# Feed-forward entry of the last two layers: where the shifts, the statistics and the turns stand in the order of the attention steps

## The reference, cut to what matters

```
h = shift_token(x)                       # upper 64 channels come from the token before
q, k, v = split(h @ wqkv); q, k = l2norm * scale, rotated
o = local_attention(q, k, v)             # windows of 64, 8 heads of 64
x = x + o @ wo
h = shift_token(x)                       # <- the feed-forward entry begins here
h = (h - mean(h)) / sqrt(var(h) + 1e-5) * lg + lb
a, g = split(h @ w1 + b1);  x = x + (a * gelu(g)) @ w2 + b2
```

## Time and profile before

| | us |
|---|---|
| median of 3 runs (lowest, highest) | 1318.48 (1316.27, 1319.15) |
| profiled execution, its own time | 1316.07 |
| span of the profiled execution | 1314.3 |
| busy: TensorE, VectorE, ScalarE, GpSimd | 1193.9, 989.3, 799.1, 387.0 |

### The profile page before, as it was taken

The page is one execution under the profiler, slowest core; times in us unless marked ns, Lnnn a source line. Parts: engine busy times, 40 slices in busy tenths (PEclk is TensorE's granted clock), DMA queues, the critical chain, the costliest instruction groups (busy, mean ns, idle before and its releaser), DMA issues.

```text
span 1314.3 us, 21968 instructions
## 1 busy us (share of the span) xinstructions
PE 1193.9 (91%) x7921; PEld 684.2 (52%) x7921; DVE 989.3 (75%) x2058; ACT 799.1 (61%) x1585; POOL 387.0 (29%) x304
## 2 busy tenths in 40 slices
PE   6799999999999879896899999998889979799987
PEld 4366666666666634342333333343567754477653
DVE  5878978889779268778566677675789857888855
ACT  5866867767768223240466666676668862688751
POOL 0000000001000035475300000014588842698823
PEclk9899999999999899996699999998989999899999
DMA  5576757767767636661323311100111100011101
GB/s 154 128 164 156 179 132 169 169 149 164 165 156 168 154 112 144 140 210 59 100 59 100 77 38 40 27 18 7 33 25 34 34 18 0 21 34 34 32 11 32
DMA packets 62824, 119.92 MB, mean 91 GB/s; under 512 B 15523, under 2 KB 30061, under 8 KB 61325
## 3 DMA queue, kind: packets, MB, share of 16 engines
q1 hardware_dynamic: 62716, 118.53, 37.6%
HBM read 37.68 MB, written 5.57 MB: 33 GB/s over the span
## 4 chain that ended last, share of the span: by engine, by line
PE 71%; DVE 14%; ACT 5%; issue 4%; POOL 2%; SPq 2%; DMA 2%; POOLq 0%; DVEq 0%; ACTq 0%
PE ps L750 15%; PE ps L770 8%; PE ps L1070 6%; PE ps L1029 5%; PE ps L1050 4%; PE ps L1127 4%; SPq L563 2%; PE ps L721 2%; PE ps L1178 2%; PE ps L1261 2%; PE ps L1200 2%; PE ps L1232 2%; ACT probsT L2260 2%; PE ps L902 2%; PE ps L892 2%
## 5 line engine op out<-in xcount | busy, mean ns | idle before, releaser
L2260 ACT ACTIVATE probsT<-ps 128x512 f32<-128x512 f32 (+1 forms) x304 | 164.0, 577 | 100.7 <-PE ps L1054 89.9
L1471 DVE TENSOR_REDUCE negmax<-ps 128x1 f32<-128x1024 f32 x128 | 153.5, 1204 | 40.6 <-PE ps L770 40.3
L2446 POOL TENSOR_SCALAR rstd<-mv 128x4 f32<-128x4 f32 (+1 forms) x31 | 7.1, 230 | 507.8 <-DVE mv L1405 507.6
L770 PE MATMUL ps<-k_st,q_st 64*128 64x512 f32 x512 | 130.7, 630 | 9.8 <-ACT d_sq L2105 5.3
L1029 PE MATMUL ps<-arena 84*128 84x512 bf16 (+3 forms) x384 | 113.7, 357 | 24.8 <-DVE cmax L1718 22.7
L2105 ACT ACTIVATE d_sq<-ps,negmax 128x1024 f32<-128x1024 f32 x86 | 95.9, 1115 | 62.1 <-DVE negmax L1471 59.4
L1718 DVE CUSTOM_DVE_ANT_0 q_st<-ps,rel 128x256 f32<-128x256 f32 (+7 forms) x128 | 96.7, 755 | 42.9 <-PE ps L1029 42.1
L750 PE MATMUL ps<-probsT,v_nat 128*128 128x256 f32 x512 | 121.3, 391 | 5.2 <-DMA probsT<-probs 3.1
L1718 DVE CUSTOM_DVE_ANT_0 k_st<-ps,rel 128x256 f32<-128x256 f32 (+7 forms) x128 | 96.8, 756 | 38.5 <-PE ps L1029 37.1
L750 PE MATMUL ps<-probsT,v_st 128*128 128x256 f32 x512 | 119.3, 385 | 1.0 <-DVE xn L1424 0.6
L1050 PE MATMUL ps<-arena 87*128 87x512 bf16 (+3 forms) x384 | 112.7, 337 | 5.5 <-ACT probsT L2260 3.3
(11 more groups left out here) (232 smaller groups left out, 2542.5 us busy)
## 6 DMA issues: line engine op xcount, KB each, us to landing
probsT<-arena SPq DMA_DIRECT2D x336, 128.0 KB, 2.4
probsT<-probs SPq DMA_DIRECT2D x176, 128.0 KB, 2.4
d_sq<-e_gates SPq DMA_DIRECT2D x16, 512.0 KB, 5.3
probsT<-probsT SPq DMA_DIRECT2D x62, 128.0 KB, 2.5
arena<-c_q_parts SPq DMA_DIRECT2D x8, 576.0 KB
arena<-c_k_parts SPq DMA_DIRECT2D x8, 576.0 KB
q_st<-e_gates SPq DMA_DIRECT2D x8, 512.0 KB, 5.2
k_st<-e_gates SPq DMA_DIRECT2D x8, 512.0 KB, 5.8
```

Of the source, the lines that this page charges most:

```text
L770: ins = pe.matmul(ps[:, pair(m, 4 + 2 * i + head) + n, :], q_st[r:r + R0, i * P:(i + 1) * P], k_st[r:r + R0, n * CH:(n + 1) * CH], start=T ...
L1471: dve.tensor_reduce(negmax[:, u:u + 1], s2, AX_X, ALU.max, negate=True).then_inc(s_a_negmax, 1)
L2260: act.activation(c_p[:, kt % 2, j0:j0 + heads, q0 - kt * P:q0 - kt * P + n], ps[:, 4 + c % 2, 0:heads * n].rearrange("p (h n) -> p h n", n ...
```

## The change

In each of the two layers (l = 0 and 1):

- VectorE: `shift` of chunks 0 and 1 moves from steps 12 and 13 to steps 10 and 11, in the same place inside the step.
- VectorE: both `ffn_stats` move from the end of step 14 to its head, before the row maximum of tile 14 (a new argument `begin`). `ffn_xn` of chunk 0 stays at the end of step 14; that of chunk 1 moves into step 15, behind nm8 of tile 15 (a new argument `early`).
- TensorE: `ffn_turn` of chunk 0 moves from ahead of step 15 to inside it (behind the scores), that of chunk 1 from inside step 15 to behind it.
- ScalarE: `ffn_yT` of chunk 0 moves inside step 15 from ahead of the copy of v to behind it (`held`), that of chunk 1 to behind the exponentials of tile 15.

No instruction is added or removed. GpSimd's and SyncE's streams stay as they are.

```diff
@@ TensorE, loop over the layers
                 ffn_in(l, 0, 0)
                 ffn_in(l, 1, 1)
                 step(l, 14)
-                ffn_turn(l, 0, 0)
-                step(l, 15, lambda: ffn_turn(l, 1, 1))
+                step(l, 15, lambda: ffn_turn(l, 0, 0))
+                ffn_turn(l, 1, 1)
                 up(l, 0)
                 up(l, 1)
                 step(l, 16)
@@ VectorE, step
-            def step(l, t, piece=None):
+            def step(l, t, piece=None, begin=None, early=None):
                     n, par = TILES * l + t, t % 2
 
+                    if begin:
+                        begin()
                     if exists(t, 2) and n:
                         rotate(l, t + 2)
...
                                                  op0=ALU.mult, op1=ALU.mult).then_inc(s_d_nm8, 1)
+                    if early:
+                        early()
                     if exists(t, -1):
                         dve.wait_ge(s_d_pt, n)
@@ VectorE, loop over the layers
-                for t in range(12):
-                    if l == 0:
+                for t in range(14):
+                    if l == 0 and t < 6:
                         step(l, t, lambda: second_batch(t))
+                    elif t in (10, 11):
+                        step(l, t, lambda: shift(t - 10, s_f_hT))
                     else:
                         step(l, t)
                 if l == 0:
                     dve.wait_ge(s_ld_d, FED)
-                step(l, 12, lambda: shift(0, s_f_hT))
-                step(l, 13, lambda: shift(1, s_f_hT))
 
                 def first_stats():
 
                     ffn_stats(l, 0)
                     ffn_stats(l, 1)
-                    ffn_xn(l, 0)
-                    ffn_xn(l, 1)
-
-                step(l, 14, first_stats)
-                step(l, 15, lambda: shift(2, s_f_hT))
+
+                step(l, 14, lambda: ffn_xn(l, 0), begin=first_stats)
+                step(l, 15, lambda: shift(2, s_f_hT), early=lambda: ffn_xn(l, 1))
                 step(l, 16)
@@ ScalarE, loop over the layers
-                def both_yT():
-
-                    ffn_yT(l, 0)
-                    ffn_yT(l, 1)
-
-                step(l, 15, both_yT)
+                step(l, 15, None, lambda: ffn_yT(l, 0))
+                ffn_yT(l, 1)
                 step(l, 16, lambda: gelu(l, 0))
```

## The result

The changed kernel took 1309.96 us (median of 7 runs, 1305.78 to 1312.43) against 1318.48 us for the kernel before (7 runs, 1315.23 to 1320.80): ratio 0.9938, 95% interval 0.9923 to 0.9954. The forecast was 1309.2 us. The execution profiled after is one of 1309.96 us, with a span of 1308.2 us.

A forecast was written before the change was run, and what follows sets the result against it. TensorE's order bounds most of the kernel, latencies the touched stretch. Saving 4.65 us a layer, 9.3 in all, takes 1316.07 to 1306.8 us; 2.4 for the median gives 1309.2 (own range 1308 to 1311; overall 1306.3 to 1313.2).

The forecast's parts named there:

- The sum: Transposes of tile 15 at 1074.6 instead of 1079.25: 4.65 us a layer, 9.3 us for two.
- Shifts at no cost: Steps 10 and 11: moved shifts cost zero, at most 0.66 us a layer; rival that they spill, 1310.5 us, chance 0.05.
- 1.9 us for the stop before `ffn_in`: TensorE's 1.77 us stop before `ffn_in` of chunk 1 goes; with pipelined transposes, worth 1.9 us.
- The statistics a draw: Head of step 14: statistics done at 1056.41, scores of tile 14 there at 1056.43, so they cost nothing.
- The path over GpSimd: Chunk 0's normalisation waits for GpSimd's power, product of tile 15 and inverse deviations, starting at 1061.44.
- What is late next: ScalarE's `ffn_yT` of chunk 1 delays `up` 0 to 1070.81; both `up`, 3.79 us, then stand on the path.
- the rival in which the change is slower: Exposed `up` at a lasting low clock: 12 us of it a layer loses 1.4 us each, 1321.3 us; chance 0.03.
- The clock: Rival: clock falls before `up` 0, losing 1.7 us a layer; 1312.6 us in both, 1310.9 in one; chance 0.15.
- the 3.56 us stop of the earlier trace: Evidence against a clock fall: products after this idle stretch took 1.95 us for four, against 3.75 after 5.60 us.
- C: First maximum of layer 1 to that of its tile 12; rest of the kernel forecast unchanged.
- A: Maximum of tile 12 to transposes of tile 15, each layer; touched stretches forecast 4 to 5 us shorter.

The follow-up runs named there:

- shifts alone: Kernel before with only the shifts of chunks 0 and 1 moved to steps 10 and 11: 1311.48 us, ratio 0.9960.
- after twice: The changed kernel and its unaltered repeat: 1309.96 us (median of 7 runs) and 1311.52 us.
- statistics at the end: Changed kernel with both statistics back at the end of step 14, ahead of chunk 0's normalisation: 1310.10 us, ratio 0.9950.
- second half: Changed kernel with chunks 2 and 3 reordered likewise on VectorE, and `ffn_in` of chunk 3 behind `up` 4 on TensorE: 1302.56 us, ratio 0.9895.
- layer change filled: Changed kernel with 22 extra mask products on TensorE in step 0 of layer 1: 1311.67 us, ratio 0.9952.
- `up` 1 behind step 16: Changed kernel with `up` 1 moved behind step 16 on TensorE: 1311.24 us, ratio 0.9940.
- with the fill: Three kernels with 7 extra mask products before `up` 0: changed kernel 1307.65 us; with chunks 2 and 3 reordered 1303.42; that plus 22 products in layer 1's step 0, 1305.37.
- before twice: The kernel before and its unaltered repeat: 1318.48 us (median of 7 runs) and 1320.87 us.
- all but the shifts: Changed kernel with the shifts put back into steps 12 and 13: 1309.16 us, ratio 0.9945 to the kernel before.
- before filled: Kernel before with 12 extra mask products on TensorE in its 3.03 us stop before `ffn_turn` of chunk 0: 1315.00 us, ratio 0.9982.

## Why the prediction was right

- **The sum.** 4.65 us a layer forecast, 4.82 and 4.84 measured. The chain came out link by link (layer 0 after, less 2.37): maximum of tile 14 at 1056.33 (forecast 1056.43), normalisation at 1061.42 (1061.44), reciprocal at 1062.70 (1062.74), `ffn_yT` of chunk 1 at 1070.03 (1070.03), `up` 0 at 1070.90 (1070.81), transposes of tile 15 at 1074.43 (1074.6). The last link is 0.17 us early because the `up` took 3.53 us back to back instead of the 3.79 of before, while `up` 0 itself began 0.09 us late.
- **Shifts at no cost.** Right: the maxima keep their pace of 8.26 us through steps 10 to 12.
- **1.9 us for the stop before `ffn_in`.** Right as a stop: the maximum of tile 14 follows that of tile 12 after 15.96 us instead of 17.96. But the shifts alone are worth 2.61 us, as nm8 also escapes GpSimd's product.
- **The statistics a draw.** Right, and more than I said: at the end of the step they cost nothing either. The path over GpSimd hides them in both places.
- **What is late next.** ScalarE in front of `up` 0, with a stop of 1.90 us against my 1.6, as forecast. Wrong was to call the two `up` the price of the change. They delay the transposes of tile 15, but from `up` 0 on TensorE is itself the bound, and with `up` 1 elsewhere the total is the same. So the rival in which the change is slower (an exposed `up` at a lasting low clock) had its premise wrong; that case itself never occurred.
- **The clock.** This is the term I mis-sized: chance 0.15, with a price of 1.7 us a layer. The price was right (1.69). Behind the stop of about 1.9 us the clock fell in 6 of 12 layers that had it (after twice, statistics at the end, second half, layer change filled, `up` 1 behind step 16), in none of 6 with the fill. In the changed kernel itself it fell in 1 of 4. The prediction named a clock below 1 behind this stop as a sign that it was wrong: the first profile of the changed kernel doesn't have it, the second has (0.57 from 1074 to 1078). The evidence against a fall was the 3.56 us stop of the earlier trace rows, which had kept the full clock. That was one outcome of several, too: in the 14 traces of this case the same stop kept the clock in 5 and was followed by the lower one in 9, here in the changed kernel's second execution:

```profile
936.33 2.43 PE L1127 MATMUL ps<-work,arena 128*128 128x512 f32 x4 [3.56 <-ACT d_sq L2290]
```

  The stretch from the first maximum of layer 0 to that of its tile 12 is 110.8 to 111.0 us in the 5 and 112.2 to 112.3 in the 9, which is part of the scatter between executions.
- **Outside the stretches.** C is the one part that I took as unchanged and that differed. In the kernel before (twice), with its stop filled and with the shifts alone it was 98.4 to 98.8 us. In the five traces that have the shifts and the new order of the turns, with the old second half and no fill at the layer change, it was 100.05 to 100.07; without the shifts 98.51, with the second half too 98.51 and 98.68. All of these carry a stop of 5.6 us with the low clock behind it; in the five the slow products reach further, and nm8 of tile 1 meets GpSimd's product. Whether the change sets the moment at which the clock comes back, or chance did, is open; five of five speak for the change. If it is the change, it gives back 1.3 us for good.

The median moved by 8.5 us (6.1 to 10.2 by the interval of the ratio). By the traces I estimate 9.7 us in the stretches, 0.7 more for the falls behind the 1.77 us stop of the kernel before (0.94 and 1.90 us in 2 of 8 layers), and 1.7 less for those before `up` 0 (half of the layers): 8.7 us, or 7.4 if C belongs to the change. The interval holds both. The mechanism is shown by the marks; that the median came within 0.8 us of the forecast is in part luck, since these items were not in the sum.

## What to carry to other kernels

Find the engine over which the path runs before you price a move: here GpSimd's power and product decided when the normalisation could start, so one of the moves was worth nothing and the two halves of the change did not add. Judge a reorder by marks inside the trace, on both sides of it; a span that scatters by several us can't tell 5 us from 3. And where TensorE stops for around two us, expect the lower clock behind it in some executions whatever one profile shows, and count it over several executions before you put a chance to it.

## What the runs showed of the hardware

- TensorE's clock falls behind the same stop in one execution and not in the next. Stops of 1.77 us: 2 of 8 layers (before twice, all but the shifts, before filled). Stops of about 1.9 us: 6 of 12. Stops of 3.03 to 3.20 us: 6 of 6. The length alone doesn't order them: at other places of the last block a stop of 1.52 us was followed by a fall in 0 of 22 cases, one of 3.3 us in 14 of 14, and one of 3.56 us in 9 of 14. Each fall was from 2.4 to 1.2 GHz and cost A 0.85 to 1.90 us. Cheap products into a free PSUM bank kept the clock up in every layer where they filled a stop of A (8 of 8).
- A small VectorE operation with both inputs in SBUF (nm8, 128x8) took 0.167 us, but 0.96 us when it met a GpSimd product of 128x512, and ended with it. GpSimd's power (128x16, 2.91 us) running at the same time did not hold it up: nm8 of tile 14 took 0.17 us at 1059.96 with the power of 1058.31 in progress, as did 26 of the 32 nm8 of the kernel before. The Trainium skill ("SBUF — State Buffer", SBUF: two separate sides) says that of a VectorE operation with two SBUF inputs and a GpSimd operation that reads SBUF the one that starts first holds the shared ports for the whole instruction, and the other is blocked. The first case agrees; the second, a GpSimd operation that reads SBUF too, does not, and the measurement decides.
